# Recurrent layers: state updates of two row groups in turns, a spread in column groups, and another order of the pieces

## The reference, cut to what matters

```python
xa = ln(x); sx = shifted(xa) - xa
xxx = tanh((xa + sx * maa_x) @ maa_w1)          # five streams of 32, then @ maa_w2
xk, xw, xv, xr, xg = xa + sx * (maa_stack + xxx)
w = exp(-exp(time_decay + tanh(xw @ td_w1) @ td_w2))
r, k, v, g = xr @ Wr.T, xk @ Wk.T, xv @ Wv.T, silu(xg @ Wg.T)
def step(s, rkvw):                               # s: a 16 x 16 state for each head
    a = k_t[..., :, None] * v_t[..., None, :]
    out = einsum('bhi,bhij->bhj', r_t, u * a + s)
    return a + w_t[..., :, None] * s, out
x1 = x + groupnorm(out) * g @ Wo.T
xc = ln(x1); sx2 = shifted(xc) - xc
y = x1 + sigmoid(xr2 @ Wfr.T) * (square(relu(xk2 @ Wfk.T)) @ Wfv.T)
```

## Time and profile before

| | |
|---|---|
| median of 3 runs | 3441.61 us (3440.38 to 3449.8) |
| the profiled execution's own time | 3439.03 us |
| its span | 3437.2 us |
| PE busy | 3294.5 us (96%) |
| DVE busy | 2639.9 us (77%) |
| ACT busy | 1860.6 us (54%) |
| POOL busy | 234.2 us (7%) |
| mean granted clock | 0.983 |

### The profile page before, as it was taken

How to read it: one execution, slowest core, us unless ns; L and a number is a source line. 1 busy time by engine, 2 the same in 40 slices (tenths; PEclk the granted TensorE clock), 3 DMA queues, 4 the chain that set the end, 5 groups by cost and what they waited for, 6 DMA issues and landing times.

```text
span 3437.2 us, 74851 instructions
## 1 busy us (share of the span) xinstructions
PE 3294.5 (96%) x31856; PEld 2491.6 (72%) x31856; DVE 2639.9 (77%) x3721; ACT 1860.6 (54%) x3086; POOL 234.2 (7%) x460
## 2 busy tenths in 40 slices
PE   5889999999999999999999999999799899998998
PEld 4667777878777787877777877777566566666666
DVE  3888888888888888888888888886546666566566
ACT  2455555555555555555545555554346656556555
POOL 1000000000000000000000000000011010010110
PEclk9999999999999999999999999999899999999999
DMA  3113323233332232332323233323244224133222
GB/s 111 62 69 111 117 93 120 93 123 111 111 111 103 104 112 101 113 119 106 123 88 119 93 108 112 109 107 120 97 110 97 66 60 115 38 84 104 56 66 53
DMA packets 91914, 336.65 MB, mean 98 GB/s; under 512 B 16704, under 2 KB 37824, under 8 KB 65600
## 3 DMA queue, kind: packets, MB, share of 16 engines
q0 software_dynamic: 39936, 234.91, 20.8%
q1 hardware_dynamic: 51216, 93.68, 8.6%
q10 hardware_dynamic: 432, 3.28, 0.2%
HBM read 252.11 MB, written 16.78 MB: 78 GB/s over the span
## 4 chain that ended last, share of the span: by engine, by line
PE 90%; DVE 6%; ACT 3%; issue 1%; DMA 0%; SPq 0%; ACTq 0%; DVEq 0%
PE psum L718 40%; PE psum L727 5%; PE psum L787 5%; PE psum L888 5%; PE psum L764 5%; PE psum L906 3%; PE psum L858 3%; PE psum L848 3%; PE psum L878 3%; DVE psum L1717 2%; PE psum L863 2%; PE psum L673 2%; PE psum L683 1%; PE psum L623 1%; PE psum L661 1%; PE psum L659 1%
## 5 line engine op out<-in xcount | busy, mean ns | idle before, releaser
L718 PE MATMUL psum<-rw 128*128 128x256 f32 x6144 | 1412.6, 386 | 14.6 <-DVE rw L1515 11.3
L718 PEld LDWEIGHTS psum<-rw 128*128 128x128 f32 x6144 | 1166.5, 193 | 227.2 <-issue 55.4
L1627 DVE TENSOR_TENSOR rw<-rw 128x2048 f32<-128x2048 f32 x192 | 429.5, 2279 | 15.0 <-ACT rw L1201 14.5
L1717 DVE CUSTOM_DVE_ANT_0 psum<-psum,mem 128x1024 f32<-128x1024 f32 x256 | 313.6, 1225 | 83.9 <-PE psum L878 83.7
L1275 ACT ACTIVATE rest<-psum,mem 128x1024 f32<-128x1024 f32 x256 | 285.1, 1114 | 80.1 <-DVE mem L1717 78.4
L888 PE MATMUL psum<-ident,rest 128*128 128x128 f32 x2048 | 269.6, 275 | 0.2 <-ACT mem L1268 0.2
L1142 ACT ACTIVATE rw<-psum 128x512 f32<-128x512 f32 x192 | 111.6, 593 | 290.7 <-PE psum L718 290.5
L1904 POOL DMA_DIRECT2D rw<-big_dram x192 | 101.9, 531 | 2382.3 <-PE psum L718 2369.8
L888 PEld LDWEIGHTS psum<-ident,rest 128*128 128x128 f32 x2048 | 235.2, 141 | 38.5 <-issue 13.1
L1509 DVE SCALAR_TENSOR_TENSOR rw<-psum,rw 128x256 f32<-128x256 f32 x480 | 196.4, 476 | 71.9 <-PE psum L673 52.9
L1080 ACT ACTIVATE rw<-rw 128x256 f32<-128x256 f32 x192 | 99.7, 590 | 271.0 <-DVE rw L1459 271.0
(11 more groups left out here) (150 smaller groups left out, 4515.0 us busy)
## 6 DMA issues: line engine op xcount, KB each, us to landing
rw<-big_dram POOLq DMA_DIRECT2D x192, 1024.0 KB, 5.1
side<-mem POOLq DMA_DIRECT2D x256, 128.0 KB, 4.3
rw<-xs_dram SPq DMA_DIRECT2D x32, 512.0 KB, 3.3
side<-mem SPq DMA_DIRECT2D x256, 64.0 KB, 2.1
rw<-rw SPq DMA_DIRECT2D x192, 64.0 KB, 1.9
xs_dram<-rw SPq DMA_DIRECT2D x24, 512.0 KB, 2.7
rw<-x_dram SPq DMA_DIRECT2D x16, 512.0 KB, 3.3
mem<-xs_dram SPq DMA_DIRECT2D x16, 512.0 KB, 4.5
```

The source lines that it names most:

```text
L718: last = mm(t[:, o * TC:(o + 1) * TC], big[:, k, P * m:P * m + P], src[:, k, 0:TC], start=k == 0, stop=k == KT - 1, skip_group_check=True)
L1627: state_dve.inc(tt(s_bd[:, half, :, :].rearrange("p c (h j) -> p c h j", h=4), own, place, ALU.mult), it, f"b{k}{half}")
L1717: maxima.inc(nc.vector.tensor_tensor_reduce(t, t, mbias.rearrange("p (a s) -> p a s", a=2), 1.0, 3.4e38, ALU.add, ALU.min, accum_out=mx[:, ...
```

## The change

Three edits, all in the recurrent part.

First, `updates` fills two tiles at once: the calls go by `n` = 0, 1 for the row groups (0, 1) and (2, 3), and inside, the products of the two row groups alternate, each into its own bank. The number of products is the same. Four calls a unit, each of 32 products, replace eight of 16. Both banks of the b ring are opened before the first product.

Second, `spread` issues 16 products of 32 weight columns instead of four of 128.

Third, the pieces are put in another order on TensorE, ScalarE and VectorE, and the ring and step lists with them. On TensorE, the first U pair of each channel pair comes before `own_outputs` and after `decay_out`; P4c and P4d now stand directly before KT0 and KT1; `fv0` moves behind the updates of pair 0; P4a and P4b come after `wo1`, VT0 and VT1 before P0a; the two `lora_two` halves and `outputs` are spaced anew; N0 goes ahead of g0 and g1, N1 stays behind them. On ScalarE `scan_inputs(0)` moves from before `fk1` to behind the KT copies, `spread_queries` behind the updates of pair 0, r1's copy behind both `group_affine`, and `s2`'s root ahead of `fr1`. On VectorE `unit_out` moves behind `mixed k`, in between the first `blocks`; `group_mean(0)` follows the second scan; `group_variance(0)`, `group_scale(0)` stand among the last `blocks`, ahead of `mixed g`.

```diff
-B_TILES = [("P0a", "dve"), ("P0b", "dve"), ("VT0", "act"), ("VT1", "act"), ("P1", "dve"), ...
+B_TILES = [("VT0", "act"), ("VT1", "act"), ("P0a", "dve"), ("P0b", "dve"), ("P1", "dve"), ...
...
             def spread(t, src):
                 for q in range(4):
-                    last = mm(t[:, 64 * q:64 * q + 64], pick[:, q, :], src, start=True, stop=True, skip_group_check=True)
+                    for g in range(4):
+                        last = mm(t[32 * g:32 * g + 32, 64 * q:64 * q + 64], pick[:, q, 32 * g:32 * g + 32], src, start=True, stop=True, skip_group_check=True)
                 return last
...
-            def updates(it, pair, q):
-                if q == 0:
+            def updates(it, pair, n):
+
+                if n == 0:
                     pe.wait_ge(vm_loaded, 16 * 4 * (2 * it + pair + 1))
                     pe.wait_ge(*b_ring.empty_at(it, "KT1"))
-                t = opened(b_ring, it, f"U{pair}{q}").rearrange("p (k j c s) -> p k c j s", k=2, j=32, c=4)
-                rows = slice(32 * q, 32 * q + 32)
+                two = (2 * n, 2 * n + 1)
+                t = [opened(b_ring, it, f"U{pair}{q}").rearrange("p (k j c s) -> p k c j s", k=2, j=32, c=4) for q in two]
+                last = [None, None]
                 for k in range(2):
                     for s in range(2):
                         for g in range(4):
                             at = 32 * g + P * k
-                            last = mm(t[32 * g:32 * g + 32, k, :, :, s], k_t[rows, s, 256 * pair + at:256 * pair + at + 32], v_m[rows, s, :, at:at + 32],
-                                      start=True, stop=True, skip_group_check=True)
-                b_ring.fill(last, it, f"U{pair}{q}")
+                            for i, q in enumerate(two):
+                                rows = slice(32 * q, 32 * q + 32)
+                                last[i] = mm(t[i][32 * g:32 * g + 32, k, :, :, s], k_t[rows, s, 256 * pair + at:256 * pair + at + 32], v_m[rows, s, :, at:at + 32],
+                                             start=True, stop=True, skip_group_check=True)
+                for i, q in enumerate(two):
+                    b_ring.fill(last[i], it, f"U{pair}{q}")
```

More of the change, by code:

```diff
@@ L116 @@
 O_TILES = [("O0", "dve"), ("O1", "dve")]
-C_TILES = [(2, "fr0", "act"), (2, "fk0", "act"), (2, "fr1", "act"), (1, "wo0", "dve"), (2, "fk1", "act"), (1, "wo1", "dve"), (2, "fv0",
-           "dve"), (1, "s1", "act"), (2, "fv1", "dve"), (1, "m1", "dve"), (1, "s2", "act"), (1, "i1", "dve")]
+C_TILES = [(2, "fr0", "act"), (2, "fk0", "act"), (2, "fr1", "act"), (1, "wo0", "dve"), (2, "fk1", "act"), (1, "wo1", "dve"), (1, "s1",
+           "act"), (2, "fv0", "dve"), (2, "fv1", "dve"), (1, "m1", "dve"), (1, "s2", "act"), (1, "i1", "dve")]
 A_DVE = ["rc", "sx", "lm", "mix_w", "mix_v", "mix_k", "mix_r", "mix_g"]
@@ L915, in _ @@
                     feed(e, "fr", 0)
+                if 0 < n and has_n:
+                    norm_a(n, "s1")
+                if has_b:
+                    values_by_token(b)
+                if has_e:
                     feed(e, "fk", 0)
@@ L950, in _ @@
                 if has_b:
-                    products(b, "P4c")
+                    products(b, "P4a")
+                    products(b, "P4b")
                 if has_n:
@@ L954, in _ @@
                 if has_b:
+                    products(b, "P4c")
                     products(b, "P4d")
-                if has_e:
-                    feed(e, "fv", 0)
-                if has_b:
                     keys_by_token(b)
@@ L961, in _ @@
                     lora_three(n, 0)
+                if has_b:
+                    updates(b, 0, 0)
+                    own_outputs(b, 0)
                 if has_c:
@@ L988, in _ @@
                 if has_b:
-                    updates(b, 1, 1)
+                    outputs(b, 0, 0)
                 if has_n:
-                    decay_in(n)
+                    lora_two(n, 0)
                     stream(n, "v", 1)
                 if has_b:
[L994 to L997, removed]
                     outputs(b, 0, 1)
[L999 to L1008, removed]
+                    updates(b, 1, 1)
                 if has_c:
@@ L1026, in _ @@
                     batch_tile(0, "v4")
+                if has_b:
+                    outputs(b, 2, 0)
+                    outputs(b, 2, 1)
                 if has_n:
@@ L1318, in _ @@
                 if 0 < n and has_n:
+                    norm_a(n, "s1")
                     norm_a(n, "sq")
+                if has_e:
+                    feed(e, "fk", 0)
+                if 0 < n and has_n:
+                    norm_a(n, "s2")
                 if has_e:
@@ L1353, in _ @@
                 if has_n:
-                    decay_in(n)
+                    decay_out(n)
+                    stream(n, "v", 0)
                 if has_b:
                     scan_inputs(b, 1)
+                    update(b, 1, 0)
+                    update(b, 1, 1)
+                if has_c:
+                    norm_c(c, "sq")
+                if s == ITS:
+                    after(0, "v1")
                 if has_n:
                     stream(n, "v", 1)
-                if has_b:
-                    update(b, 1, 0)
-                    update(b, 1, 1)
-                if has_n:
-                    decay_out(n)
                 if has_b:
@@ L1369, in _ @@
                 if has_c:
-                    norm_c(c, "sq")
+                    norm_c(c, "s2")
                 if s == ITS:
-                    after(0, "v1")
-                if has_n:
-                    stream(n, "k", 0)
+                    after(0, "v2")
                 if has_b:
@@ L1384, in _ @@
                     square(0, 1)
-                if has_c:
-                    norm_c(c, "s2")
-                if s == ITS:
-                    after(0, "v2")
+                if has_b:
+                    group_square(b, 0)
                 if has_n:
+                    stream(n, "k", 1)
                     stream(n, "r", 0)
+                if has_b:
+                    group_deviation(b, 0)
                 if has_c:
@@ L1804, in _ @@
                 if has_e:
+                    unit_out(e, 0)
+                if has_b:
+                    blocks(b, 0, 0)
+                if has_e:
                     unit_out(e, 1)
@@ L1834, in _ @@
                     blocks(b, 3, 1)
-                if has_c:
-                    norm_c(c, "xn")
+                    group_scale(b, 0)
                 if has_n:
@@ L1852, in _ @@
                 if has_b:
-                    gated(b, 0)
                     gated(b, 1)
```

120 lines of the change are left out of this document (53 added, 67 removed).

## The result

The kernel after takes 3424.4 us (median of 5 runs, 3421.6 to 3429.59), the kernel before 3442.57 (median of 5). The ratio of after to before is 0.9947, 95% interval 0.9932 to 0.9962: 0.5% faster, 18 us, where 39 us were forecast. The profiled execution took 3429.59 us, the slowest of the five; its span is 3427.8.

A forecast was written before the change was run, and what follows sets the result against it. TensorE's queue was taken as the bound: 3.4 us less work minus 1.7 of new waits saves 1.7 a step, 41 over 24 steps, taken as 39: 3400 us profiled, median 3403. Own range 3380 to 3420, wide range 3355 to 3442.

The forecast's parts named there:

- rival B: Recurrent part: the handovers eat the whole gain, waits of 3.4 us a step, 3440 us; chance 0.14.
- TensorE's own work: TensorE's queue in the recurrent part: shorter by 3.4 us a step, 3.0 from updates and 0.4 from spread.
- The updates: Update tiles on TensorE: four alternating calls of 1.03 us replace 7.1 us a unit, saving 3.0 us.
- The spread: `spread` in norm_a and norm_c on TensorE: 1.78 us falls to 1.2 to 1.4, 0.4 us less.
- rival C: In `updates`: alternating row groups don't run side by side, 1.9 us a call, 3468 us; chance 0.10.
- KT: TensorE at KT0 and KT1 waits for VectorE to empty the banks of P4c and P4d: 0.5 us a step.
- lora_three 1: TensorE at lora_three 1 waits for the end of the first mixing on VectorE: 0.6 us a step.
- updates(0, 1): This update call opens both banks and waits for ScalarE to copy both first tiles: 0.1 us a step.
- g0: TensorE at g0 waits for VectorE's mixed g, VectorE becoming the bound there: 0.6 us a step.
- the walk along ScalarE: ScalarE from first scan's end to U10 and U11 copies: some 12.5 us, 0.7 us before TensorE needs it.
- The clock: TensorE's time at the lower clock level, whole span: the new order may move it 5 to 10 us either way.
- A: Recurrent part: nothing new waits, VectorE's margins being better than laid out, 3357 to 3370 us; chance 0.20.

The follow-up runs named there:

- spread_alone: The kernel before with only the second edit, `spread` in 16 products: 3426.67 us, ratio 0.995.
- lora_split: root_after_gate with lora's second half moved behind P4c and P4d: 3397.51 us, ratio 0.9861.
- g_first: lora_split with mixed g ahead of group_scale(0) on VectorE, N0 between g0 and g1, affine and gating of pair 0 later: 3381.06 us, ratio 0.9811.
- root_after_gate: The kernel after with ScalarE taking fr1's sigmoid ahead of s2's root again, as before: 3403.68 us, ratio 0.9882.
- updates_alone: The kernel before with only the alternating update calls, spread and order as before: 3513.33 us, ratio 1.0202.
- updates_and_spread: The kernel before with both product edits in the old order, so the kernel after without its third edit: 3439.32 us, ratio 0.9982.
- lora_two_late: updates_and_spread with lora_two 0 behind updates(1, 1) instead of ahead of it: 3406.83 us, ratio 0.9888.

## Why the prediction was wrong

The direction was right, and the size was less than half: 18 us for 39. The time lies outside the forecast's own 3380 to 3420 us and inside the wide range, between the forecast and rival B. At full clock a step lost 0.56 us where 1.7 were forecast.

*TensorE's own work.* Forecast 3.4 us a step. Adding the 2.5 us of waits to what the step really lost gives 3.1 (98.33 - 97.77 + 2.5). The updates gave about 2.8 for 3.0. The call was taken at 1.03 and is 1.09; the first of the two doubles was taken at 1.54 and takes 1.63 to the next piece (1595.95 to 1597.58), so that the sum before is 7.2, not 7.1. The 0.13 us for the ends of a stretch that this part assumes stands in no row. The spread alone gave 0.28 for 0.4 (spread_alone). The overlap of row groups itself was read rightly from the 1.54 us of a doubled tile, and rival C fell: 64 records start within 1.09 us, 17 ns each. The floor of about 25 ns that the Trainium skill states ("TensorE: Matmul & The Clock Gate", section "Wait — 56ns, not 53.3ns?") does not hold here for products in different tiles of the array.

*The waits that were forecast.* KT 0.38 (0.5), lora_three 1 0.54 (0.6), updates(0, 1) none (0.1), g0 0.66 (0.6). They stood where the text put them, and lora_split and g_first took two of them away for 0.61 and 0.42 us a step.

*The step that failed* is the walk along ScalarE: "some 12.5 us in all, by my layout 0.7 us before TensorE needs it". The row from the first scan's end to U11's copy was priced by summing durations of rows of before, in whose order the exponential needs no table load, and only its end was held against TensorE. The moved root changed which table was in place at the exponential, and 1.28 us fell into exactly this row: from the carry to U11's copy it takes 13.2 us (1596.17 to 1609.33), against 11.6 without the load in root_after_gate (1586.41 to 1598.03). The end still held, as updates(1, 1) waits for nothing. What came too late were two handovers in the middle of the row, for which the forecast has no wait: decay_out's exponential for lora_two 0 and the copy of v0 for v1. They cost 0.9 us a step. Undone, the time is 3403.68. The text listed "s2's root ahead of fr1" among the moves and gave it no price. Without the load both handovers are in time, though v0's copy now stands behind decay_out on ScalarE, a move that the list of the change doesn't name.

*The clock* was put at 5 to 10 us either way. It gave back 17 us in the twenty steps and took as much elsewhere: outside them the profiled execution has 119.5 us at half clock, the one of before 82.7. In time, from the start to the first update it is +3.6 us, from the last unit's first update to the first scores +8.8, in the untouched attention part +4.5, with 20.5 us at half clock against 11.0. Within the +8.8 lies one wait of `own_outputs` for group_mean(0), 7.6 us where it was 2.5; why it grew was not tested. The balance: twenty steps -25.2, the ends and the three other steps +15.8, -9.4 us between the two profiled spans. The medians differ by 18 us, since the profiled execution of after lies 5 us above its median and that of before 4 below. So over the whole execution the clock stayed within the 5 to 10 us, and the forecast's error is in the length of the step: 1.1 us a step, some 27 us in 24, of which the clock in the medians gave a part back.

*The rivals.* A fell (2.5 us of waits). B, everything eaten, was nearest in its mechanism: ScalarE's row was 1.3 us longer by the load, where B asks for 2, and it was v1 and lora_two 0 that slipped, not updates(1, 1).

Open: which piece makes TensorE's clock fall. In updates_alone, updates_and_spread and lora_two_late the half-clock stretches that were looked at follow narrow products with waits. But waits are not needed: in its twenty steps the kernel before has nine stretches, 34.1 us in all, and TensorE waits for nothing there. One of them (window, columns as above) follows the lora_two 0 and update tiles of 1221.02 to 1224.10:

```profile
1225.00:1228.00 3.00, 3.00 (x8) 2.38 (x8) 2.60 (x2) 1.41 (x2) 0.00 (x0) 0.50 0.00 0
```

And waits are not enough, as the kernel after has four in nearly every step and no stretch. With equal products the order decides between 0 and 81.9 us of them in twenty steps (the kernel after, updates_and_spread), and between 68.3 and 204.8 without the new spread. What the rule is, the runs don't show.

## What to carry to other kernels

When pieces of ScalarE are moved, write beside each piece the table that it needs, before and after. Here the load saved at tanh came back at the exponential, and it cost 0.85 us a step because others wait for that row. When a long row of one engine is walked, hold each handover in it against the engine that waits, and not only its end. A gain in the length of one engine counts only where that engine doesn't wait anyhow: the same edit brought 0.34 us a step in an order with four waits and 1.14 in one with a single wait, so remove the waits first and count the gain afterwards. Judge an edit of TensorE's queue with the granted clock of each stretch beside it.

## What the runs showed of the hardware that was not expected

A kernel whose TensorE work is shorter by about 2.8 us a step became 2% slower by the clock (updates_alone): 10.2 us at 1.2 GHz in each of twenty steps, at the same places, and each step 102.4 us long to within 0.1. Such a pattern can go on from step to step: in updates_and_spread two steps of 102.2 us were followed by eighteen of 98.9, each with a single low stretch. The order of the kernel after, in steps of nearly the same work, had none.

Products of 32 x 32 weights and 128 columns in eight tiles of the array (four column groups, two row groups, two banks) start every 17 ns on average, both ends of the stretch in it; in four tiles of one row group it is 31 ns (32 records in 1.00 us).
